# Denominator sums moved behind the second tile's logits in a linear attention kernel

## The reference

```python
qh = softmax(Wq @ layernorm(x), axis=head_dim) * SCALE     # per head and position
kh = softmax(Wk @ ctx, axis=position)
vh = Wv @ ctx
context = einsum('bhdn,bhen->bhde', kh, vh)
out = einsum('bhde,bhdn->bhen', context, qh)
out = Wo @ out + bo                                        # then divided by its norm, scaled by g
x = x + tanh(g_xattn) * out
x = x + tanh(g_ffn) * ffn(layernorm(x))                    # gate and up of 1376, silu, down
```

## Time and profile before

| | |
|---|---|
| time of the kernel, median of 3 runs | 683.95 us (682.94 to 685.32) |
| the profiled execution: time, span | 683.78 us, 682.0 us |
| mean granted TensorE clock | 0.994 of full speed |
| steps 2 to 15 of the attention | 335.44 us of the span |
| one step | 23.89 us (step 8) |
| busy: PE, DVE, ACT, POOL | 656.4, 587.1, 466.2, 378.0 us |

### The profile page before, as it was taken

One profiled execution on the slowest core, in us unless ns is written; L12 is line 12 of the kernel. 1 busy time (PEld: TensorE's weight loads), 2 busy tenths in 40 slices (PEclk: granted clock), 3 DMA queues, 4 the chain that ended last, 5 costly groups with the idle time before them and its releaser, 6 DMA issues.

```text
span 682.0 us, 14635 instructions
## 1 busy us (share of the span) xinstructions
PE 656.4 (96%) x5141; PEld 342.0 (50%) x5141; DVE 587.1 (86%) x785; ACT 466.2 (68%) x822; POOL 378.0 (55%) x448
## 2 busy tenths in 40 slices
PE   6899999999999999999999998999999999999995
PEld 5554555455455545545554533444444544454443
DVE  7778898898889888888988468999999999989987
ACT  4786677678777767877776756667766766666663
POOL 6212333333343433334345486798788877887885
PEclk9899999999999999999999999999999999999999
DMA  4112330430332132022111100000010001000102
GB/s 116 36 41 65 98 88 17 102 95 19 86 95 62 41 83 79 16 74 79 57 30 25 26 6 2 1 1 2 0 40 23 1 1 47 17 1 16 47 0 63
DMA packets 32047, 28.98 MB, mean 42 GB/s; under 512 B 20047, under 2 KB 22234, under 8 KB 32002
## 3 DMA queue, kind: packets, MB, share of 16 engines
q1 hardware_dynamic: 29594, 27.73, 14.8%
q10 hardware_dynamic: 2408, 0.70, 0.4%
HBM read 22.42 MB, written 4.23 MB: 39 GB/s over the span
## 4 chain that ended last, share of the span: by engine, by line
PE 81%; ACT 8%; DVE 4%; POOL 3%; issue 2%; DMA 1%; SPq 1%; ACTq 0%; POOLq 0%; DVEq 0%
PE pair L1200 8%; PE pair L1410 8%; PE small_pair L1121 8%; ACT eq L721 7%; PE pair L1411 7%; PE small_pair L1087 7%; PE pair L1073 6%; PE pair L1434 4%; PE small_pair L1105 4%; PE pair L1446 4%; PE small_pair L1410 4%; PE small_pair L1411 4%; PE pair L1052 3%; PE pair L1210 2%; PE pair L1185 2%
## 5 line engine op out<-in xcount | busy, mean ns | idle before, releaser
L1804 DVE SCALAR_TENSOR_TENSOR acc<-pair,scale_T,acc 128x512 f32<-128x512 f32 (+1 forms) x176 | 131.7, 748 | 15.2 <-ACT acc L864 2.0
L621 POOL TENSOR_TENSOR yT<-yT,y_scaled 128x512 f32<-128x512 f32 (+1 forms) x78 | 100.5, 1290 | 4.3 <-ACT y_scaled L889 3.5
L712 ACT ACTIVATE ek<-pair,kneg 128x512 f32<-128x512 f32 x128 | 86.5, 683 | 19.0 <-DVE kneg L1672 19.0
L1410 PE MATMUL pair<-ek,w_gu 128*128 128x512 f16 (+1 forms) x235 | 91.3, 389 | 1.5 <-DVE acc L1804 1.2
L1411 PE MATMUL pair<-ekT,w_gu 128*128 128x512 f16 (+1 forms) x235 | 89.0, 379 | 0.0
L1677 DVE TENSOR_TENSOR eq<-eq,pair 128x1024 f32<-128x1024 f32 x64 | 77.7, 1215 | 9.8 <-PE pair L1185 9.3
L1667 DVE TENSOR_REDUCE qmax<-pair 128x16 f32<-128x1024 f32 x64 | 78.2, 1222 | 7.8 <-PE pair L1052 7.2
L721 ACT ACTIVATE eq<-pair 128x1024 f32<-128x1024 f32 x64 | 65.7, 1026 | 21.5 <-PE pair L1210 21.5
L1672 DVE TENSOR_REDUCE kneg<-pair 128x2 f32<-128x1024 f32 x64 | 77.9, 1217 | 0.5 <-PE pair L1073 0.5
L1434 PE MATMUL pair<-in_hi,d_int 128*128 128x512 f32 (+1 forms) x132 | 75.8, 575 | 1.2 <-DVE yT L1843 1.2
L599 POOL TENSOR_TENSOR inter<-act_gate,acc 128x512 f32<-128x512 f32 (+1 forms) x43 | 55.2, 1284 | 39.0 <-DVE acc L1804 15.4
(11 more groups left out here) (206 smaller groups left out, 1427.8 us busy)
## 6 DMA issues: line engine op xcount, KB each, us to landing
xall<-in_x SPq DMA_DIRECT2D x16, 256.0 KB, 2.7
ctx_raw<-in_ctx SPq DMA_DIRECT2D x16, 256.0 KB, 2.9
out_x<-xall SPq DMA_DIRECT2D x16, 256.0 KB, 2.0
zero<-zeros_plus SPq DMA_DIRECT2D x8, 344.0 KB, 5.3
packed<-in_L_ffn_gate_qweight SPq DMA_DIRECT2D x4, 688.0 KB
packed<-in_L_ffn_up_qweight SPq DMA_DIRECT2D x4, 688.0 KB
packed<-in_L_ffn_down_qweight SPq DMA_DIRECT2D x10, 256.0 KB
zero<-zeros_plus SPq DMA_DIRECT2D x5, 256.0 KB, 5.0
```

Of the source, the lines that this page charges most:

```text
L621: pool.tensor_tensor(yT16[:, nt, :] if it == IT - 1 else total, total, y_scaled[:, nt, :], ALU.add).then_inc(z_add, 1)
L712: act.activation(ek[:, b, t, :], k_pairs[t % 2][:, b, :], ACT.Exp, bias=kneg[:, b, t:t + 1], scale=-1.0, accum_out=ksum[:, k_slot(b, t):k_ ...
L1410: pe.matmul(gu_bank[count % 3][0:w, :], lhsT, xT_hi[:, g, rows], start=True, stop=False)
L1804: dve.scalar_tensor_tensor(out=acc[0:w, n % 2, m, :], in0=gu_bank[(8 * n + job) % 3][0:w, :], scalar=scale_T[0:w, it, 4 * m + g:4 * m + g ...
```

## The change

On TensorE, `denominators()` is called behind `t_logits(1)` and `k_logits(1)` instead of ahead of them, so that the second tile's logits come directly behind the first tile's and the denominators directly ahead of the outputs. On ScalarE, the copy of the denominators comes behind the first two key exponentials instead of ahead of them. Both hold for steps 2 to 15; steps 0, 1 and 16 keep their order. VectorE, GpSimd and SP are unchanged.

```diff
@@ ScalarE, step @@
-                denominators()
                 if not residual:
+                    denominators()
                     k_transposed(3, back=1)
                 k_exps(0)
-                if not residual:
+                if residual:
+                    denominators()
+                else:
                     gates()
                 if not last:
                     x_high(p + 1, 1 - par)
```

## The result

The changed kernel takes 699.8 us in the median (699.51 to 702.26, four runs) against 683.93 us (682.94 to 685.32, four runs) for the kernel before: ratio 1.0238, 95% interval 1.0209 to 1.0268. It is slower by 15.9 us; 701.2 us, 17.4 more, was forecast.

The account below looks back on a forecast made before the run. TensorE's chain was taken to bound each step, with the denominators' path through copy, transfers and reciprocal within a fifth of a microsecond. 14 steps x 1.24 us = 17.4 us on 683.8 gave 701.2 us, range 697 to 705.

Parts of the forecast that it names:

- TensorE stands 0.32 us for the first maximum: TensorE, second tile's logits: start at 196.15 after VectorE's first maximum, TensorE free at 195.83, so a 0.32 us wait.
- The denominators start 1.45 us late, and so does the copy: TensorE, behind the second tile's logits: denominators start at 197.28 instead of 195.83, shifting the sum's path by 1.45 us.
- The copy's place behind the exponentials is free: ScalarE: the two key exponentials end at 198.61, the copy's sums come at 199.21, so they cost nothing, by 0.60 us.
- The transfers take what they took: SP's four denominator transfers: durations as in step 8 before, so the reciprocal starts at 204.02 instead of 202.57.
- Rival A: Transfers land sooner, so only TensorE's 0.32 us gap is paid in each of 14 steps: 4.5 us, 688.3 us; chance 0.05.
- B: Rival: the later transfers land late in every step, as in step 5 before: 714.7 us; chance 0.06.
- 0.2 us of lateness is free, the rest is paid in full by every later operation: VectorE's third maximum, behind the reciprocal: 1.24 us late, and later operations with it; 14 steps, 17.4 us.
- Rival C: Faster: VectorE's order of work sets the step's end, its 0.39 us wait before the second maximum comes off: 678.3 us; chance 0.03.

Follow-up runs that it names:

- the additional transfer: Kernel before plus one unread 8 KB transfer that SP issues ahead of the four, steps 2 to 15: 690.31 us; same on the changed kernel: 731.98 us.
- the output product moved ahead: Kernel before with the first output product between the first tile's query and key logits: 692.06 us; same with transfers split over two queues: 690.76 us.

## Why the prediction was right

- *TensorE stands 0.32 us for the first maximum.* Measured: the second tile's logits wait 0.26 us in the timeline's row, since they followed the maximum's end by 0.05 us and not by 0.12; the sum did not use it. With the landing out of the way the changed order costs 4.4 us, put at 4.5.
- *The denominators start 1.45 us late, and so does the copy.* Measured in step 8: 1.42 and 1.41, the reciprocal 1.42.
- *The copy's place behind the exponentials is free.* Right for the changed kernel: ScalarE waits 0.56 us for the sums in front of it (0.60 forecast), and its old place wins nothing (699.55). Alone it costs 8.3 us (9.1 expected of that run).
- *The transfers take what they took.* From the copy's end to the reciprocal 4.22 us (212.13 less 207.91) against 4.21. Rival A's earlier landing didn't come, nor B's late ones; step 5, whose landing had been late, was not late again.
- *0.2 us of lateness is free, the rest is paid in full by every later operation.* The 14 steps were 1.22 us longer in the mean (1.24 forecast). The third maximum was 1.30 us late in step 8, since it followed its reciprocal by 1.05 us there; in most of the steps it was the 0.96 that the forecast took from step 5. The other runs give the same slack: the reciprocal of step 8 was 0.71 us late with the additional transfer, 0.74 with ScalarE's part alone, 0.83 with the output product moved ahead, and 1.44 with TensorE's part alone; they cost 0.47, 0.59, 0.58 and 1.20 us a step, always 0.15 to 0.25 less.
- *Rival C*, VectorE's 0.39 us coming off, fell: its time ahead of the reciprocal became wait, 34.7 us for 14.2.

The sum of the terms, 17.4 us, met the 17.1 us of the steps. What the forecast of 701.2 us missed against the median of 699.8 is mostly outside the changed steps: it started from one profiled execution of the kernel before, whose steps begin at 49.96 us. In the profile of TensorE's part alone (700.12 us) they begin at 49.16. The kernel before had medians of 682.8 to 683.9 us beside the experiments; against 682.79, TensorE's part alone came to 16.8 us more.

## What to carry to other kernels

An engine that idles in front of a landing may still be on the tight path: ask what is queued behind the waiting instruction, and look for a step in which the same landing happened to be late. When a block is moved to bring another forward, price what the moved block feeds, here five microseconds of copy, transfers and reciprocal, before what it unblocks. If a path through small transfers is the tight one, issue them from two queues: here that alone took 12.4 us of the 16.8 back, but look at what runs on GpSimd at the time to which the work behind the landing moves.

## What the runs showed of the hardware

- Four transfers of 8 KB issued by SP took 2.82 us of issuing, 0.64 to 0.72 each, and the last landed 2 us behind the start of its issue (210.12 to 212.11 in step 8); from two queues, 1.54 and 1.33 us at the same time.
- VectorE's small SBUF operations stood while a GpSimd operation of 1.26 to 1.29 us, begun shortly before, ran, and ended 0.05 to 0.08 us behind it: the 128x64 cast took 1.04 us instead of 0.20, the subtraction 1.21 instead of 0.23. The Trainium skill's page "SBUF — State Buffer", section "Who interferes with whom", says that GpSimd contends for a port pair with a VectorE cast that runs in a two-port mode, or with a VectorE operation that has two SBUF inputs if GpSimd's reads SBUF, and that the second waits for the whole of the first; these rows agree, though no run shows the mode of the cast. The changed kernel runs 0.3 us clear of it (its last small operation ends at 213.26 in step 8, GpSimd's begins at 213.60), so that a transfer of 0.67 us more, 9.4 us by itself, brought the collision and the clock with it and cost 32 us.
- TensorE's clock kept 2.4 GHz through waits of 0.8 to 1.0 us in each step of the changed kernel. It fell to 1.2 GHz behind 5 of 10 waits of 2.6 us in one run, and behind 2 of 14 waits of 1.5 to 1.7 us in another. Where it fell, the step took 1.5 to 2.9 us longer than its neighbours with the same wait.
